# Masks of the last query half on VectorE, chunk 2's rows behind the last normalisation, expert words behind rows 3 and 7

## What is computed

```python
h = layernorm(x) * (1 + ca) + sa
x = x + ga * attention(h)            # causal: scores of later keys are -inf, softmax, @ v, @ W_out
h = layernorm(x) * (1 + cb) + sb
cw = top 4 of 16 experts (from the best 2 of 4 groups) by softmax(h @ gate_w.T), normed to 1
out = sum over e of cw[:, e] * (silu(g_e) * u_e @ expert_down_w[e].T)   # g_e, u_e = h @ expert_up_w[e].T
x = x + gb * (out + silu(g) * u @ shared_down_w.T)
```

## Time and profile before

| what | us |
| --- | --- |
| median of three runs | 633.43 (631.21 to 637.81) |
| the profiled execution's own time | 630.09 |
| its span | 628.4 |
| PE busy | 576.8 (92%) |
| DVE busy | 477.5 (76%) |
| ACT busy | 373.5 (59%) |
| POOL busy | 341.5 (54%) |

### The profile page before, as it was taken

The page is one execution under the profiler, slowest core; times in us unless marked ns, Lnnn a source line. Parts: engine busy times, 40 slices in busy tenths (PEclk is TensorE's granted clock), DMA queues, the critical chain, the costliest instruction groups (busy, mean ns, idle before and its releaser), DMA issues. The chain is left out here.

```text
span 628.4 us, 13726 instructions
## 1 busy us (share of the span) xinstructions
PE 576.8 (92%) x3945; PEld 390.7 (62%) x3945; DVE 477.5 (76%) x1406; ACT 373.5 (59%) x877; POOL 341.5 (54%) x646
## 2 busy tenths in 40 slices
PE   4997899999999999998987798898979999999987
PEld 4885543334343434443342387687869999999964
DVE  4968998888898778686948569799756776667767
ACT  4775576666676656555867564454546666666630
POOL 5114563646567554944648877781345555555550
PEclk9989999999999999997999989999999999999999
DMA  8389669864547480751115143774986444444983
GB/s 288 82 208 247 179 147 221 206 174 109 141 100 219 117 220 26 174 215 55 69 52 187 54 170 121 252 217 140 339 341 198 139 131 130 137 139 137 355 311 125
DMA packets 66083, 107.96 MB, mean 172 GB/s; under 512 B 13513, under 2 KB 52185, under 8 KB 63834
## 3 DMA queue, kind: packets, MB, share of 16 engines
q1 hardware_dynamic: 59146, 87.93, 48.5%
q0 software_dynamic: 6864, 19.15, 7.9%
HBM read 60.90 MB, written 43.88 MB: 167 GB/s over the span
## 5 line engine op out<-in xcount | busy, mean ns | idle before, releaser
L1458 ACT ACTIVATE Pr<-bank 128x512 f32<-128x512 f32 (+3 forms) x384 | 165.7, 494 | 97.9 <-PE bank L2261 94.1
L1574 DVE TENSOR_REDUCE mxA<-bank 128x1 f32<-128x128 f32 (+3 forms) x256 | 112.3, 482 | 20.9 <-PE bank L2148 20.6
L2261 PE MATMUL bank<-Qs,Ks 99*128 99x512 bf16 (+3 forms) x384 | 118.0, 331 | 6.0 <-ACT Pr L1458 4.2
L2148 PE MATMUL bank<-Ks,Qs 96*128 96x512 bf16 (+3 forms) x384 | 120.2, 330 | 1.2 <-DVE mxB L1574 0.6
L1280 POOL DMA_INDIRECT expert_rows<-Y,YIX x79 | 77.3, 978 | 78.5 <-ACT Y L1521 75.4
L1574 DVE TENSOR_REDUCE mxB<-bank 128x1 f32<-128x512 f32 x128 | 81.6, 681 | 13.8 <-PE bank L2148 13.8
L2247 PE MATMUL bank<-Pr,Vst 128*32 128x512 f32 (+3 forms) x768 | 83.0, 505 | 3.5 <-POOL Pr L1259 3.5
L1257 POOL TENSOR_TENSOR tick<-ident 128x1 f32<-128x1 f32 x128 | 25.5, 199 | 106.5 <-ACT Pr L1458 105.6
L2506 PE MATMUL bank<-W,xh 128*128 x316 | 78.0, 328 | 1.1 <-issue 1.1
L1209 POOL DMA_INDIRECT chosen_rows<-Hx,pos x64 | 67.6, 1056 | 19.2 <-issue 19.2
L2261 PEld LDWEIGHTS bank<-Qs,Ks 99*128 99x128 bf16 x384 | 35.9, 98 | 58.4 <-ACT Pr L1458 39.3
(11 more groups left out here) (256 smaller groups left out, 1278.3 us busy)
## 6 DMA issues: line engine op xcount, KB each, us to landing
G<-chosen_rows SPq DMA_DIRECT2D x79, 134.0 KB, 2.2
Z<-expert_rows SPq DMA_DIRECT2D x8, 1024.0 KB, 8.3
W<-expert_words SPq DMA_DIRECT2D x7, 1088.0 KB, 9.5
qk_parts<-AP SPq DMA_DIRECT2D x32, 192.0 KB, 3.1
Wraw<-in_wexp SPq DMA_DIRECT2D x9, 608.0 KB, 5.7
SA<-in_wexp SPq DMA_DIRECT2D x7, 608.0 KB, 4.3
Vst<-Vall SPq DMA_DIRECT2D x8, 512.0 KB, 5.3
expert_words<-SH SPq DMA_DIRECT2D x7, 480.0 KB, 3.6
```

Of the source, the lines that this page charges most:

```text
L1458: nc.scalar.activation(Pr[(2 * s + j // 2) % 4][:, j % 2, 0:w], ebank[p % RING][:, 0:w], ACT.Exp, scale=SCALE).then_inc(exp_done, EXP)
L1574: nc.vector.tensor_reduce(dst, mbank[u % RING][:, 0:w], AX.X, ALU.max).then_inc(m_red, 1)
L2148: nc.tensor.matmul(mbank[u % RING][:, 0:w], Qs[slot][0:NPR, i // TPC, j, (i % TPC) * P:(i % TPC + 1) * P], Ks[slot][0:NPR, j, k0:k0 + w], ...
L2261: nc.tensor.matmul(ebank[p % RING][:, 0:CH - q0], Ks[slot][0:NAUG, j, kt * P:(kt + 1) * P], Qs[slot][0:NAUG, qc, j, q0:CH], start=True, st ...
```

## The change

Four edits, all in one version.

1. **Masks.** In the last group, steps 8 to 11 are masked by VectorE: it takes, in place, the minimum of each 128 x 128 square of the exponentials with a tile that holds 3.0e38 where the key is not later than the query and 0 elsewhere. GpSimd makes this tile once (in PADZ, after its zeros have been stored), in group 4. GpSimd's eight masks of these steps, with their `tick` instructions, are gone, and it goes on with sends: three more of chunk 1 stand in step 8.
2. **Chunk 2.** VectorE's `rows` of chunk 2 stand behind the last normalisation instead of under the last steps of attention; the low parts of experts' words 3 and 4 stand ahead. TensorE's transposes of these rows and its logits stand one shared piece later each, its counts too.
3. **Chunk 3.** Its statistics stand behind the third shared product instead of ahead of it, and `route` of chunk 3 is cut: the part from SEL_DONE on stands behind the product of piece 7.
4. **Words.** SP issues the words 11 to 13 behind the rows of block 3 and 14 to 17 behind those of block 7, where it was behind blocks 7 to 12.

```diff
+def masked_by_vector(n, s):
+
+    return n == NIT - 1 and STEPS[s][0] == S // CH - 1
 POST_PE = {
-    -1: [("h", 2, 0), ("h", 2, 1), ("turn_out",)], 0: [("ta", 3, 0), ("ta", 3, 1), ("lg", 2)],
-    1: [("pj", 3, 0), ("pj", 3, 1), ("px", 2)], 5: [("h", 3, 0), ("h", 3, 1)], 6: [("lg", 3)], 8: [("px", 3), ("cnt",)],
+    -1: [("turn_out",)], 0: [("h", 2, 0), ("h", 2, 1), ("ta", 3, 0), ("ta", 3, 1)],
+    1: [("lg", 2), ("pj", 3, 0), ("pj", 3, 1)], 2: [("px", 2)], 5: [("h", 3, 0), ("h", 3, 1)], 6: [("lg", 3)], 8: [("px", 3), ("cnt",)],
 POST_ACT = {
-    -1: [("h", 2, 0), ("h", 2, 1), ("xh", 1)], 0: [("ta", 3, 0), ("ta", 3, 1), ("exp", 2)], 3: [("hi", 5), ("xh", 2)], 4: [("h", 3, 0), ("h", 3, 1)], 5: [("exp", 3)], 8: [("hi", 6), ("xh", 3)], 11: [("hi", 7)],
+    -1: [("xh", 1)], 0: [("h", 2, 0), ("h", 2, 1), ("ta", 3, 0), ("ta", 3, 1), ("exp", 2)], 3: [("hi", 5), ("xh", 2)], 4: [("h", 3, 0), ("h", 3, 1)], 5: [("exp", 3)], 8: [("hi", 6), ("xh", 3)], 11: [("hi", 7)],
-    (7, 7): [("send", 0, 14, 16)], (7, 8): [("send", 1, 0, 1)],
+    (7, 7): [("send", 0, 14, 16)], (7, 8): [("send", 1, 0, 4)], (4, 4): [("least",)],
-    -1: [("send", 1, 1, 16)], 1: [("send", 2, 0, 2), ("root", 3), ("send", 2, 2, 16)], 9: [("send", 3, 0, 16)],
+    -1: [("send", 1, 4, 16)], 1: [("send", 2, 0, 2), ("root", 3), ("send", 2, 2, 16)], 9: [("send", 3, 0, 16)],
-    (7, 4): [("route", 1, SEL_DONE, POS_DONE)], (7, 6): [("ta", 2, 0), ("ta", 2, 1)], (7, 7): [("res", 2, 0)],
-    (7, 8): [("res", 2, 1)] + [(what, 2, t) for what in ("stats", "aggr") for t in range(TPC)],
-    (7, 9): [("xl", 0), ("lo", 3)], (7, 10): [("rows", 2, t) for t in range(TPC)], (7, 11): [("lo", 4)],
+    (7, 4): [("route", 1, SEL_DONE, POS_DONE)], (7, 6): [("ta", 2, 0), ("ta", 2, 1), ("lo", 3)], (7, 7): [("res", 2, 0)],
+    (7, 8): [("lo", 4)], (7, 9): [("res", 2, 1)] + [("stats", 2, t) for t in range(TPC)],
+    (7, 10): [("aggr", 2, t) for t in range(TPC)], (7, 11): [("xl", 0)],
-    -1: [("norm", 15), ("xl", 1)], 0: [("soft", 2)], 0.5: [("route", 2, 1, PLACED)],
+    -1: [("norm", 15)] + [("rows", 2, t) for t in range(TPC)] + [("xl", 1)], 0: [("soft", 2)], 0.5: [("route", 2, 1, PLACED)],
-    1.5: [(what, 3, t) for what in ("stats", "aggr") for t in range(TPC)],
-    2.5: [("rows", 3, t) for t in range(TPC)], 3: [("xl", 2)], 5: [("soft", 3), ("route", 3, 1, POS_DONE)],
-    8: [("tot",)], 9: [("xl", 3)], 10: [("lo", 5)], 13.5: [("tab",)],
+    2: [(what, 3, t) for what in ("stats", "aggr") for t in range(TPC)],
+    2.5: [("rows", 3, t) for t in range(TPC)], 3: [("xl", 2)], 5: [("soft", 3), ("route", 3, 1, SEL_DONE)],
+    7: [("route", 3, SEL_DONE, POS_DONE)], 8: [("tot",)], 9: [("xl", 3)], 10: [("lo", 5)], 13.5: [("tab",)],
-BLOCK_SP = {7: [("final", 11), ("final", 12)], 9: [("final", 13)], 10: [("final", 14), ("final", 15)], 11: [("final", 16)], 12: [("final", 17)]}
+BLOCK_SP = {3: [("final", 11), ("final", 12), ("final", 13)], 7: [("final", 14), ("final", 15), ("final", 16), ("final", 17)]}
+            def least_kept():
+
+                pool.wait_ge(pad_kept, 16 * 4)
+                nc.gpsimd.memset(PADZ[:, 0:P], LARGE).then_inc(pad_made, 1)
+                pool.wait_ge(pad_made, PADS_MADE + 1)
+                nc.gpsimd.affine_select(out=PADZ[:, 0:P], in_=PADZ[:, 0:P], compare_op=ALU.is_ge, fill=0.0,
+                                        base=0, pattern=[[1, P]], channel_multiplier=-1).then_inc(pad_made, 1)
-                    if on_diagonal(s):
+                    if on_diagonal(s) and not masked_by_vector(n, s):
+            def mask_pair(n, s, pair):
+
+                dve.wait_ge(exp_done, n * (EXP * HEADS) + EXP * (HG * s + 2 * pair + 2))
+                dve.wait_ge(pad_made, PADS_MADE + 2)
+                v = Pr[(2 * s + pair) % 4][:, :, 0:P]
+                nc.vector.tensor_tensor(v, v, PADZ[:, 0:P].unsqueeze(1).broadcast_to([P, 2, P]), ALU.min).then_inc(masked, 1)
+                        if on_diagonal(s) and masked_by_vector(n, s):
+                            for pair in range(HG // 2):
+                                mask_pair(n, s, pair)
```

More of the change, by code:

```diff
@@ L74 @@
 MAGIC = float(3 * 2 ** 22)
+LARGE = 3.0e38
 SLOTS = 3
@@ L1245, in work @@
                     make_pads()
+                if what == "least":
+                    least_kept()
             def body(n, at, first, last):
```

## The result

The changed kernel takes 636.63 us (median of 20 runs, 632.20 to 639.51), the kernel before, in runs between them, 631.27 (20 runs, 627.72 to 637.81). The ratio on record is 1.0078, 95% interval 1.0058 to 1.0097: 4.9 us slower, between 3.7 and 6.1. It is not formed as the quotient of the two medians, which is 1.0085 here and lies inside the interval. The profiled execution of the changed kernel has a span of 634.7 us, 6.3 more than that of before.

What follows compares the result with a forecast made beforehand. Bound by VectorE's shared-expert steps, then transfers of words and rows, then TensorE's blocks from 468 us. Row 8's late landing +2.3 and clock +1.3 gave +3.6 us on the 633.4 median: 637.0 us, range 631.0 to 642.5.

Steps and rivals of the forecast that it cites:

- The likeliest case: The main forecast: late shared expert, row 8 waiting behind words, and a clock loss; +3.6 us, chance 0.55.
- Masks: End of attention: masks on VectorE let TensorE's last output transposes start at 360.4 instead of 363.81 us.
- Rows of chunk 2 behind: After the last normalisation: TensorE waits 1.7 us for these rows; softmax of chunk 2 comes 2.3 us later.
- Behind it: Shared expert after chunk 2's softmax: delay passes on, softmax of chunk 3 +2.6 us, blocks start +1.7.
- later still: Rival: clock falls ahead of late rows and queue keeps 0.317 MB per us; row 8 after 463.5, 642.2 us, chance 0.13.
- Sends, SP: Chunk 3's last send goes 3.3 us later; SP's first row transfer moves from 430.44 to 433.7 us.
- Words: SP's queue in the blocks: turn 4 about a microsecond late, turn 8 waits almost five; costs +2.3 us.
- Clock: TensorE's idle time at turn 8 lowers its clock; costs +1.3 us, between 0 and 1.5.
- What 5.2 us there were to win: Blocks' turns 10 to 15: 5.2 us lost before the change, as rows land late behind experts' words.
- Rows not held behind words: Rival: rows 4 to 15 land in 2.1 us despite the words; -3.5 us, 629.9 us, chance 0.15.
- one queue: Forecast's reason for late rows: one engine's transfers share a ring in each DMA engine, taken in ring order.
- Shared expert not late: Rival: VectorE's pauses absorb the +3.3 us, row 8 lands at 457.4; sum about 0, 633.4 us, chance 0.12.

Runs made afterwards that it cites:

- after_even: Changed kernel, but words 11 and 12 issued behind block 3's rows, then one expert behind each of blocks 7, 8, 9, 10, 12; 0.9979 against before.
- no_words: Changed kernel with the order of words put back as before, so masks, chunk 2 and chunk 3 edits only; 1.0014 against before.
- after_words_act: Changed kernel with the seven experts' words issued by ScalarE in a queue of its own, in place of the new word order; 1.0025 against before.
- words_alone: Kernel before with only the change's new word order (11 to 13 behind block 3's rows, 14 to 17 behind block 7's); 1.0024 against before.
- words_last: Kernel before with words 11 and 12 behind block 3's rows, 13 to 15 behind blocks 7 to 9, 16 behind 11, 17 behind 13; 0.9913 against before.
- masks_rows: Kernel before with only the masks edit and the chunk 2 edit; chunk 3's statistics, its route and the words as before; 1.0022 against before.
- words_even: Kernel before with words 11 and 12 behind block 3's rows, then one expert behind each of blocks 7, 8, 9, 10, 12; 0.9898 against before.
- words_act: Kernel before with the seven experts' words issued by ScalarE in a queue of its own, only rows in SP's; 0.9993 against before.
- masks_alone: Kernel before with only the masks edit, VectorE's other work left where it was; 1.0030 against before.
- words_spread: Kernel before with words 11 and 12 behind block 3's rows, 13 and 14 behind block 7's, 15 to 17 behind blocks 8 to 10; 0.9949 against before.

## Why the prediction was right or wrong

The time came out right, 637.0 forecast and 636.63 measured, but the median of before was 631.27 with more runs, not 633.43; so the effect was forecast at +3.6 and is +4.9 (3.7 to 6.1). That the two times lie 0.4 us apart is luck: the median of before came out 2.2 us lower, and the difference of the medians (5.4 us) 1.8 larger than the forecast's +3.6. The likeliest case is the one that came. Step by step, counted from the first mark:

- *Masks.* Right. Last products 1.7 and 2.6 us earlier (forecast 1.6 and 2.4), the last output's transposes 3.7 (3.4).
- *Rows of chunk 2 behind.* Right. TensorE waits 1.68 us (1.7 forecast), the softmax of chunk 2 is 1.9 later (2.3).
- *Behind it.* Mis-sized. Rows of chunk 3 +2.5 (forecast +2.7, with a root wait of 1.26 for 1.0), but the softmax of chunk 3 is +4.0, not +2.6. The step said that TensorE's wait of two microseconds is gone. That one is, but VectorE's late rows made another, 2.11 us, which the forecast had not looked for, and at 395 to 400 us the clock was 0.66: from the transposes of these rows to the logits it took 4.53 us (393.87 to 398.40), before 3.09. That is the excess of 1.4 us. after_even has edit 3 too, but its low stretch came earlier (383 to 388 us) and filled that wait: there the transposes come as late as in the changed kernel (36.45 and 36.41 us behind the first mark), and the softmax of chunk 3 is +2.5, close to the forecast's +2.6. no_words and after_words_act have the +4.0 and a low stretch ahead of the logits as the changed kernel has. So the step's excess is one low stretch in front of the logits. It is what the rival "later still" said, at another wait; that rival was to be told by row 8 landing after 463.5 us, and turn 8 starts at 464.60, or 463.0 without the 1.6 us ahead of the first mark, between the two cases.
- *Sends, SP.* +4.0 and +4.3 us, forecast +3.3 each, by the same excess. The first turn is +2.7 (forecast +1.7).
- *Words.* The mechanism was right (waits move from turns 11 to 13 to turns 4 and 8), the split was not: 3.69 and 2.94 us, forecast one and almost five. Data were taken to start 2.0 us behind an issue and to move at 0.40 MB per us with the row landing at once behind them. From the words' true issue at 438.48 that gives 449.2 us for row 4; TensorE had it at 451.8. In words_alone it gives 443.5 against 445.6, so three experts' words hold a row 2 to 2.6 us longer than counted. Row 8, by the forecast's count shifted by the same 2.8 us, is due 463.5, and turn 8 came at 464.6. What turn 4 lost, turn 8 no longer had to.
- *Clock.* Wrong term. Behind the 3.69 us the clock was 0.89 over 450 to 465 us and turn 5's transposes took 0.64 instead of 0.41 us. But turns 4 to 7 took 7.66 us, before 7.48: it cost 0.2 us, not 1.3. The forecast's B was 36.2 + 0.6 + 1.3 = 38.1 us and 38.13 was measured, the second part of it for a wrong reason: it is turn 4's row.
- *What 5.2 us there were to win.* Right, and confirmed from the other side: words_last takes 30.78 us for B, 5.4 below before. At the end of its trace 3.1 us of it were left (and its ratio says 5.5, between 3.2 and 7.7).
- *Rivals.* Rows not held behind words: refuted for this order by words_alone and after; that rows wait for bytes is shown by words_last. But the forecast's reason, one queue, was too narrow: with two queues they wait as long. Shared expert not late: refuted (A +2.7).

Still open: the ratios put edits 1 to 3 at +0.9 (no_words), +1.4 (masks_rows) and, as differences of ratios, some +3 to +5 us (changed kernel against words_alone, after_even against words_even), each with an interval of about 2 us either way or more. Where a low stretch falls may decide which, and one trace of each kernel doesn't say how often it falls where.

## What to carry to other kernels

Order transfers by the latest time at which each is needed, and count for every small urgent one the megabytes that are under way when it is issued; issuing bulk "as early as possible" only moves the waits to the front, in one queue or in two. When work moves to an engine that others wait for, follow the displaced piece to its reader: 3.7 us won at the end of attention came back as a wait for the rows that had made room. A forecast that ends at the right total can do so with two terms wrong; only a cut of the trace at common marks shows it, and the cut has to go on to the end, where a gain can be lost again.

## What was unexpected of the hardware

- A second hardware queue gave small transfers no precedence in words_act: 134 KB in 9.3 us beside 1088 KB transfers of another queue, against 3.3 us in one queue with the large ones issued later.
- The first mark lay between 352.80 and 358.67 us in fourteen traces whose code up to there is nearly the same. One part of it is where the low clock falls: from the positions of chunk 1 (near 342 us) to the first mark it took 13.56 or 13.57 us in nine traces (and 13.9 in masks_alone, whose masks come late) and 14.7 to 14.8 in four, in which PEclk was 0.89 from 340 to 355 us. Three of these four have all of edits 1 to 3 (the changed kernel, no_words, after_words_act; after_even, with them too, has 13.57), one has none of them (words_spread), and masks_rows, whose code is the same up to there, has 13.57. So whether the changed kernel's +1.6 us at the first mark belongs to the change in part stays open.
- A low stretch came without an idle piece right ahead of it. In the changed kernel's trace TensorE was busy 5.00, 4.97 and 4.79 of 5 us (as the profile counts it) while the clock went from 1.00 to 0.50; the last idle piece listed before, 1.10 us, ended at 314.55 us. In the trace of before the clock stayed at 1.00 from 315 to 330 us.

```profile
315.00:320.00 5.00, 5.00 (x39) 2.19 (x36) 3.39 (x6) 3.86 (x10) 1.64 (x6) 1.00 0.00 0
320.00:325.00 5.00, 4.97 (x42) 2.74 (x40) 2.38 (x9) 2.25 (x9) 2.54 (x7) 0.84 0.27 108
325.00:330.00 5.00, 4.79 (x25) 1.10 (x24) 0.25 (x2) 3.08 (x8) 4.42 (x11) 0.50 0.15 55
```

- A low stretch may cost nothing: at 383 to 388 us in after_even it used up time in which TensorE would have waited for VectorE, and the transposes behind it came as late as in the changed kernel.
